# A two-stage transformer block in split fp32 on one Trainium2 core: 33 row pairs instead of 34, a re-ordered sort, two re-ordered quads, an early gelu table and a last store from ScalarE's queue

## The reference

```python
# layer 0, x: (64, 64, 512); H = 2048
q, k, v = x @ Wq, x @ Wk, x @ Wv
attn = softmax(einsum('btd,bTd->btT', q, k) * 512 ** -0.5)
attn_out = einsum('btT,bTd->btd', attn, v) @ Wp + bp
cms_out = gelu(attn_out @ cW1 + cb1) @ cW2 + cb2 + one_hot(target)[:, None, :]
modifier = gelu(concat([attn_out, cms_out]) @ mW1 + mb1) @ mW2 + mb2
x = clip(x + cms_out + modifier, 0, 1)
# layer 1, one of three roles for each batch, K = 256
h = gelu(x @ W_down[role] + b_down[role])
y = x + h @ W_up[role] + b_up[role]
out = layernorm(y) * gamma[role] + beta[role]
```

## Time and profile before

| | us |
|---|---|
| median of three runs | 2051.75 (2050.34 to 2052.19) |
| the profiled execution | 2051.32 |
| its span | 2049.7 |
| TensorE busy | 2010.7 (98%) |
| VectorE busy | 1396.4 (68%) |
| ScalarE busy | 952.6 (46%) |
| GpSimd busy | 109.3 (5%) |
| mean granted clock of TensorE | 0.997 |

### The profile page before, as it was taken

The page is one execution under the profiler, slowest core; times in us unless marked ns, Lnnn a source line. Parts: engine busy times, 40 slices in busy tenths (PEclk is TensorE's granted clock), DMA queues, the critical chain, the costliest instruction groups (busy, mean ns, idle before and its releaser), DMA issues.

```text
span 2049.7 us, 28141 instructions
## 1 busy us (share of the span) xinstructions
PE 2010.7 (98%) x9396; PEld 1674.5 (82%) x9396; DVE 1396.4 (68%) x2598; ACT 952.6 (46%) x1980; POOL 109.3 (5%) x202
## 2 busy tenths in 40 slices
PE   8999999999999999999999999999999999999996
PEld 6878888888878888888878888888878888888896
DVE  6686786555777686556686786565686685654996
ACT  4754453433654444333564453333474454342664
POOL 0000000000000000000000000000000000000132
PEclk9999999999999999999999999999999999999998
DMA  4121233315211143125111233224211222222754
GB/s 165 32 62 42 72 124 108 93 56 196 63 51 62 52 144 108 57 83 206 62 52 52 62 129 98 72 93 185 83 51 42 73 98 93 93 88 88 235 160 107
DMA packets 113408, 194.32 MB, mean 95 GB/s; under 512 B 12457, under 2 KB 72370, under 8 KB 108788
## 3 DMA queue, kind: packets, MB, share of 16 engines
q1 hardware_dynamic: 98772, 128.81, 20.1%
q0 software_dynamic: 14496, 63.72, 9.0%
HBM read 148.97 MB, written 43.52 MB: 94 GB/s over the span
## 4 chain that ended last, share of the span: by engine, by line
PE 85%; DVE 7%; SPq 2%; DMA 2%; ACT 2%; issue 2%; DVEq 0%; POOL 0%; ACTq 0%; POOLq 0%
PE y L1663 15%; PE y L1665 15%; PE y L1664 15%; PE x L1663 13%; PE x L1665 13%; PE x L1664 13%; DVE w_lo L1105 1%; PE y L1744 1%; SPq L452 1%; DVE f L1229 1%; PE x L1769 1%; SPq L460 1%; DVE a_forms L1274 1%; DMA w_blocks<-w1c 1%; DMA bet<-beta 1%
## 5 line engine op out<-in xcount | busy, mean ns | idle before, releaser
L683 ACT CAST w_hi<-w_blocks 128x512 fp32r<-128x512 f32 (+1 forms) x464 | 231.6, 519 | 132.5 <-PE y L1665 84.1
L1105 DVE TENSOR_TENSOR w_lo<-w_blocks,w_hi 128x512 fp32r<-128x512 f32 (+1 forms) x464 | 249.7, 564 | 56.2 <-ACT w_hi L683 56.2
L1663 PE MATMUL x<-h_hi,w_hi 128*128 128x512 f32 x512 | 199.6, 390 | 3.8 <-ACT f L736 3.8
L1663 PE MATMUL y<-h_hi,w_hi 128*128 128x512 f32 x512 | 199.7, 390 | 1.9 <-ACT p_copy L736 1.9
L1664 PE MATMUL x<-h_lo,w_hi 128*128 128x512 f32 x512 | 199.3, 389 | 0.0
L1665 PE MATMUL x<-h_hi,w_lo 128*128 128x512 f32 x512 | 199.2, 389 | 0.0
L1665 PE MATMUL y<-h_hi,w_lo 128*128 128x512 f32 x512 | 199.2, 389 | 0.0
L1664 PE MATMUL y<-h_lo,w_hi 128*128 128x512 f32 x512 | 199.2, 389 | 0.0
L1663 PE MATMUL y<-a_forms,w_hi 128*128 128x512 f32 x480 | 188.1, 392 | 2.2 <-DVE f L1208 1.2
L1665 PE MATMUL y<-a_forms,w_lo 128*128 128x512 f32 x480 | 186.8, 389 | 0.0
L1664 PE MATMUL y<-a_forms,w_hi 128*128 128x512 f32 x480 | 186.8, 389 | 0.0
(11 more groups left out here) (227 smaller groups left out, 4265.8 us busy)
## 6 DMA issues: line engine op xcount, KB each, us to landing
w_blocks<-w1m SPq DMA_DIRECT2D x128, 256.0 KB, 4.6
w_blocks<-w1c SPq DMA_DIRECT2D x64, 256.0 KB, 3.2
w_st<-w2c SPq DMA_DIRECT2D x64, 256.0 KB, 3.0
w_st<-w2m SPq DMA_DIRECT2D x64, 256.0 KB, 4.7
x_hi_lo<-x_halves POOLq DMA_DIRECT2D x6, 2048.0 KB, 11.1
zs<-z_by_batch SPq DMA_DIRECT2D x68, 128.0 KB, 2.1
cms<-f SPq DMA_DIRECT2D x32, 256.0 KB, 2.7
z_cms<-cms POOLq DMA_DIRECT2D x8, 1024.0 KB, 7.1
```

The source lines that it names most:

```text
L683: nc.scalar.copy(w1_hi[:, w % RING, cols], src).then_inc(w1_hi_s, 1)
L1105: nc.vector.tensor_tensor(w1_lo[:, w % RING, cols], src, f32(w1_hi[:, w % RING, cols]), ALU.subtract).then_inc(w1_lo_s, 1)
L1663: nc.tensor.matmul(ps, w[0], x[0], start=first, stop=False, skip_group_check=more)
```

## The change

Five edits.

1. Pairs. An odd batch of a role among the first 48 no longer pads its group; it moves to the group of the same role among the last 16. `NPAIR` goes from 34 to 33. The sort gets ten more small instructions. Its list is also cut in three: `sort_halves` stays, `sort_starts` goes behind two copies of the second weight product, `sort_slots` goes behind the first query tile, and `onehot_bias` goes from ahead of the first `inverse` to behind the first `split_v`.
2. The start. The first row of the first weight product takes its four hi x hi matmuls first, and these wait for the hi halves alone.
3. The two second quads. In the opening quad VectorE takes `sum_p6` and `sum_p7` ahead of P3's weight split, then `block22`, `hidden_lo` of the last C12 (until now in the attention), `block21`, and `block12` right behind the first weight split of the next quad; its `weight_sums` go forward in the attention, and ScalarE takes gelu C11 ahead of the next quad's splits. In the second quad of mW1 TensorE takes P1, P6, P7, P5 instead of P1, P5, P7, P6.
4. The gelu table. ScalarE runs one gelu of a column of 128 constants near the end of each attention. The second layer of the first quad waits for gelu C21 only where it first writes C21's bank (column block 3).
5. The last store of first rows is issued by ScalarE's queue instead of GpSimd's.

```diff
-NPAIR = B // 2 + 2 * (R // 2)
+NPAIR = B // 2 + R // 2
@@ sync, store_second
-                sp.wait_ge(a_stored[u % UNROLL], (n - u % UNROLL) * (16 // UNROLL) + 16)
+                if n == NPAIR - 1:
+                    sp.wait_ge(last_a, 16)
+                else:
+                    sp.wait_ge(a_stored[u % UNROLL], 16 * (n // UNROLL + 1))
@@ gpsimd: store_first for all pairs but the last
-            for n in range(NPAIR):
+            for n in range(NPAIR - 1):
@@ scalar, quad
                 if Q % (2 * NQ) == 1:
                     copy_p1(Q)
                     split_q(Q, P3)
+                    gelu(Q, C11)
...
-                if q:
+                if q and Q % (2 * NQ) != 1:
                     gelu(Q, C11)
@@ scalar, attention
                 output(m - 1)
+                if s == 0:
+                    act.wait_ge(mhalf_s, 1)
+                nc.scalar.activation(warm[:], mhalf[:], ACT.Gelu)
                 output_hi(m - 1)
@@ scalar, end
+            b = act.value_load(first_t[0:1, NPAIR - 1:NPAIR], min_val=0, max_val=B - 1)
+            act.wait_ge(yo_s, NPAIR)
+            act.dma_start(out[bass.ds(b, 1)].rearrange("o s d -> (o s) d"),
+                          yo[0:S, (NPAIR - 1) % UNROLL, :]).then_inc(last_a, 16)
+            act.wait_ge(last_a, 16)
@@ vector, sort_halves: +3 instructions; sort_slots: +7
+                link(nc.vector.tensor_scalar(count[:, 0:R], sort_bank[0:B, NG:NG + R], -1.0, None, ALU.add))
...
+            def sort_starts():
                 link(nc.vector.memset(start[:, 0:1], 0.0))
...
@@ vector, quad
-                if q:
-                    split_q(Q, P3)
                 if opening:
                     sum_p6(Q)
                     sum_p7(Q)
+                if q:
+                    split_q(Q, P3)
                 if opening or not q:
                     block22(Q)
+                if opening:
+                    hidden_lo(Q - 1, C12)
+                    block21(Q)
                 if (Q + 1) % NQ or Q // NQ % 2 == 0:
                     weight_sums(Q + 1)
...
                 split_next(Q, 0)
+                if opening:
+                    block12(Q)
@@ vector, attention
+                    if s == 0 and c == 0:
+                        sort_slots()
...
-                    onehot_bias()
...
                 split_v(m0)
+                if s == 0:
+                    onehot_bias()
...
                 hidden_lo(Q, C11)
+                weight_sums(Q + 1)
                 hidden_lo(Q, C21)
...
-                weight_sums(Q + 1)
...
-                hidden_lo(Q, C12)
@@ tensor, weight_product
+                    if ready + k == 0:
+                        for seen, x, y in (((qw_hi, 2), 0, 0), ((qw_lo, 1), 1, 0), ((qw_lo, 2), 0, 1)):
+                            pe.wait_ge(*seen)
+                            for m in range(DC):
+                                nc.tensor.matmul(banks[m][:], lhs[:, x, k, m * P:(m + 1) * P], rhs(k)[y],
+                                                 start=x + y == 0, stop=False)
+                        continue
@@ tensor, quad
-                for k, first_seen in zip((P1, P5, P7, P6), seen):
+                begin = list(zip((P1, P5, P7, P6), seen))
+                if q == 1 and g % 2:
+                    begin = [begin[n] for n in (0, 3, 2, 1)]
+                for k, first_seen in begin:
@@ tensor, second1
-                if q == 0:
-                    pe.wait_ge(*((part_s, 4 * Q) if g % 2 else (gelu_s, 4 * Q + C21 + 1)))
+                if q == 0 and g % 2:
+                    pe.wait_ge(part_s, 4 * Q)
...
+                        if Q % (2 * NQ) == 0 and j == 0 and c == 3:
+                            pe.wait_ge(gelu_s, 4 * Q + C21 + 1)
```

More of the change, by code:

```diff
@@ L99 @@
 NG = 2 * R
-NPAIR = B // 2 + 2 * (R // 2)
+NPAIR = B // 2 + R // 2
 NSLOT = 2 * NPAIR
+SLOTS_KNOWN = 8 + (2 * NG + 3) + NG + 11
 UNROLL = 4
@@ L144, in program @@
         ones2 = sb("ones2", [P, P], F32R)
+        warm = sb("gelu_table", [P, 1])
         mx = sb("mx", [P, 1])
@@ L181, in program @@
             half = sb("half", [B, NG], on=sorting)
+            count = sb("count", [B, NG], on=sorting)
+            spare = sb("spare", [B, R], on=sorting)
+            moved = sb("moved", [B, R], on=sorting)
+            shift = sb("shift", [B, R], on=sorting)
             start = sb("start", [B, NG], on=sorting)
@@ L332, in program @@
         rstd_s, yg_s, yo_s = sem("rstd"), sem("times_gamma"), sem("row_ready")
+        last_a = sem("last_first_stored")
         a_stored = [sem(f"first_stored{k}") for k in range(UNROLL)]
@@ L1067, in sort_halves @@
                 dve.wait_ge(sort_mm, 2)
+                link(nc.vector.tensor_scalar(count[:, 0:R], sort_bank[0:B, NG:NG + R], -1.0, None, ALU.add))
                 for r in range(NG):
-                    link(nc.vector.tensor_scalar(flags[:], even[:], sort_bank[0:B, NG + r:NG + r + 1], None, ALU.is_lt))
+                    if r == R:
+                        link(nc.vector.scalar_tensor_tensor(out=spare[:], in0=half[:, 0:R], scalar=-2.0, in1=count[:, 0:R],
+                                                            op0=ALU.mult, op1=ALU.add))
+                        link(nc.vector.scalar_tensor_tensor(out=count[:, R:NG], in0=spare[:], scalar=1.0,
+                                                            in1=sort_bank[0:B, NG + R:2 * NG], op0=ALU.add, op1=ALU.add))
+                    link(nc.vector.tensor_scalar(flags[:], even[:], count[:, r:r + 1], None, ALU.is_lt))
                     link(nc.vector.reduce_sum(half[:, r:r + 1], flags[:], AX_X))
-            def sort_slots():
+            def sort_starts():
                 link(nc.vector.memset(start[:, 0:1], 0.0))
@@ L1077, in sort_slots @@
                                                         in1=start[:, r - 1:r], op0=ALU.mult, op1=ALU.add))
+            def sort_slots():
                 link(nc.vector.tensor_tensor(rank_r[:], sort_bank[0:B, 0:NG], start[:], ALU.add))
+                link(nc.vector.scalar_tensor_tensor(out=rank_r[:, R:NG], in0=spare[:], scalar=1.0, in1=rank_r[:, R:NG],
+                                                    op0=ALU.add, op1=ALU.add))
+                link(nc.vector.scalar_tensor_tensor(out=moved[:], in0=half[:, 0:R], scalar=-2.0,
+                                                    in1=sort_bank[0:B, 0:R], op0=ALU.mult, op1=ALU.add))
+                link(nc.vector.tensor_scalar(moved[:], moved[:], 0.0, None, ALU.is_ge))
+                link(nc.vector.tensor_tensor(shift[:], start[:, R:NG], start[:, 0:R], ALU.subtract))
+                link(nc.vector.scalar_tensor_tensor(out=shift[:], in0=half[:, 0:R], scalar=-2.0, in1=shift[:],
+                                                    op0=ALU.mult, op1=ALU.add))
+                link(nc.vector.tensor_tensor(shift[:], shift[:], moved[:], ALU.mult))
+                link(nc.vector.tensor_tensor(rank_r[:, 0:R], rank_r[:, 0:R], shift[:], ALU.add))
                 link(nc.vector.tensor_tensor(rank_r[:], rank_r[:], onehot[:], ALU.mult))
@@ L1305, in quad @@
                 split_pre(pre_block(Q, 1))
-                block21(Q)
+                if not opening:
+                    block21(Q)
                 hidden_lo(Q, C11)
                 split_next(Q, 3)
-                block12(Q)
+                if not opening:
+                    block12(Q)
                 hidden_lo(Q, C21)
@@ L1557, in _ @@
             sort_halves()
-            sort_slots()
             for j in (0, 2):
@@ L1561, in _ @@
                 nc.vector.tensor_copy(h1_tile[:, j, :], Y[j][:]).then_inc(wa_out, 1)
+            sort_starts()
             for s in range(NS):
@@ L1693, in sort_gather @@
             def sort_gather():
-                pe.wait_ge(sort_v, 8 + 2 * NG + 1 + (NG - 1) + 4)
+                pe.wait_ge(sort_v, SLOTS_KNOWN)
                 for v in range(3):
@@ L1759, in output @@
                 if m == 0:
-                    pe.wait_ge(sort_v, 8 + 2 * NG + 1 + (NG - 1) + 5)
+                    pe.wait_ge(sort_v, SLOTS_KNOWN + 1)
                 elif p == 0:
```

5 lines of the change are left out of this document (2 added, 3 removed).

## The result

The changed kernel takes 2032.84 us (median of 4, 2032.40 to 2032.96), the kernel before beside it 2051.21: a ratio of 0.9907, 95% interval 0.9894 to 0.9919, 18.4 us less. The forecast was 2035.8, 2032.0 to 2041.5. The profiled executions have spans of 2049.7 and 2030.8: 18.9 less, where the sum of the forecast was 15.75 (some 0.8 of the 18.9 goes with slow load issues in the one execution of the kernel before that was profiled; see "One pair less").

What follows compares the result with a forecast made beforehand. TensorE, busy for 98% of the span, bounds the kernel, so only fewer matmuls or shorter waits help. Seven items sum to 15.75 us off 2051.3, giving 2035.6, stated as a median of 2035.8; range 2032 to 2041.5.

Steps and rivals of the forecast that it cites:

- Items 1 and 2: Start and sort: first matmuls wait for hi halves only, 0.8 us; sort links moved behind copies and query tile, 1.25 us.
- Item 3: Gelu table loaded early near each attention's end, and `second1`'s wait moved to bank 3: 0.6 us a step, 2.4 in all.
- the rival of a load twice as long: Gelu table load holds ScalarE 2 x 1.28 us: item 3 is -0.9, time 2038.9; chance 0.03.
- Item 4: Opening quad: two TensorE waits save 4.4 and 4.0 us, P5 of the next quad gives back 3.0: 5.4.
- The rival in which nothing comes back: Opening quad: `part` additions run ahead as in later quads, so item 4 is 8.4 us, time 2032.8; chance 0.2.
- Item 5: mW1's second quad: P6 and P7 ahead of P5 remove its wait for `block12`: 1.5 us, bounds 0.9 and 1.5.
- P6 and P7 first give it 5.4 us: mW1's second quad: running P6 and P7 first gives P5's wait for `block12` 5.4 us.
- The rival "slower": mW1's second quad: a ScalarE and VectorE chain behind P5 exceeds 8.2 us, deciding from 4 us excess; time 2057, chance 0.03.
- Item 6: Pairs: one fewer saves 3.6 us of TensorE plus SyncE's lag of 0.25: 3.85, between 3.3 and 3.9.
- the last pair's load is late: End of the pairs: waits run through SyncE's queue, and TensorE stands 0.60 + 0.16 us for the last load.
- Item 7: Last store of first rows on ScalarE's queue instead of GpSimd's: 0.55 us less, bounds 0 and 0.7.
- ScalarE should be like SyncE: 0.15 + 2.3 = 2.45: Last store: ScalarE's store was to start and land like SyncE's, 2.45 us instead of 3.0.

Runs made afterwards that it cites:

- One pair less: Follow-up on the changed kernel with one filler pair more, 34 again, all else as changed: 2036.56 us, ratio 0.9918 to the kernel before.
- the undone start: The changed kernel with the first row of the first weight product as before, waiting for the lo half of Wk: 2033.45 us, ratio 0.9912.
- the store alone: The kernel before with only the last store of first rows moved from GpSimd's queue to ScalarE's: 2048.47 us, ratio 0.9982.
- the old opening quad: The changed kernel with VectorE's and ScalarE's order for the opening quad of each cW1 stage as before: 2043.75 us, ratio 0.9955.
- the late lo half: The changed kernel with the opening quad's `hidden_lo` of C21 behind the next quad's `part` additions: 2031.10 us, ratio 0.9895 to the kernel before.

## Why the prediction was right, and where it was not

**Items 1 and 2** came out at 2.11 where the sum has 2.05, but not by their own terms. The first matmul is at 6.38 and not 6.2, and the undone start shows that its gain is within the spread of the clock's rise. The 0.98 at the first query tile is the earlier copies (32.53, so 1.06 earlier, where 1.3 was counted), and that tile still waits (0.43). The 1.0 at 57.43 was 1.07: this step of item 2 holds. The 0.15 that `onehot_bias` was to cost shows as 0.12 at the first output, behind the place where the 2.11 is read. No run undoes the sort's order by itself, so item 2 rests on these rows.

**Item 3** was 0.72 in each step by the offset at `second1` (0.6), and 2.70 over the stretches from the step before to P4, in which up to 0.14 is lost ahead of it. The early gelu runs 0.02 behind the end of a load of 1.28 (92.08 + 1.28, and 93.38), so the rival of a load twice as long is out. The Trainium skill ("ScalarE: Activation LUTs", What ACT_TABLE_LOAD costs) adds a drain of about 1.38 to each load; neither this row nor what follows it shows one: the gelu stands at 93.38, and ScalarE's next cast starts at 93.49.

**Item 4** had its mechanism right: the two waits gave 9.01 (8.4), and P5 of the next quad gave 2.77 back (3.0), with `part` as releaser, as named. The chain from `sum_p6` to the end of `part` takes 125.18 - 113.52 = 11.7, as forecast. By the offsets P4's wait is worth 1.04 in each step, 4.2 (4.4), and the second one 4.8 (4.0). The forecast had taken 0.4 off the latter for bank 3; that loss is real, but shows in the give-back: of the 2.77, 0.5 is bank 3, and P1 and P5 gave back 2.2, where 2.6 had been put on them. The rival in which nothing comes back names 2032.8, which is the measured time, but it is not what happened: the 2.77 came back, and other items made up for it.

**Item 5** failed. The step "P6 and P7 first give it 5.4 us" holds, and P5's wait is gone from the list, worth 0.47 in each step, 1.9. But nothing was said of P4, which comes behind P5, `second1` and P2. It waits for `sum_p7`, behind weight sums that wait for a DMA, and it took 1.05 and 0.43 back in two steps. 0.36 was left. The rival "slower" looked at this chain, but only from P5's side; its excess of 4 us never came.

**Item 6** was 4.62 (3.85): 3.7 for the pair, where 3.6 was counted, and some 0.8 for the last load's wait, of which the forecast took 0.25. The step "the last pair's load is late" read one execution as the rule: with the store alone, 34 pairs have no such wait, so the change itself is worth about 3.7.

**Item 7** was right in sign for a wrong reason. The step "ScalarE should be like SyncE: 0.15 + 2.3 = 2.45" failed: the store is issued 0.18 behind the row and lands 2.9 later, and SyncE's own store is issued at 2025.4, 3.1 behind the last row, where it was 3.0 before. That term is nothing. 2.87 came from GpSimd's drain, which the forecast had as "the closing wait of 5.8 to the end" and kept fixed. That row named TensorE's sequencer as the releaser, whose own closing instruction starts at 2034.2 and takes 1.2; the engine named had long been done, so another one held the end, and the forecast did not ask which.

Forecast 15.75, measured 18.9: item 7 gave 2.3 more, item 4 0.8, item 6 0.8, item 3 0.3 more, item 5 1.1 less. Items 3, 5, 6 and 7 all lie outside their own bounds, item 7 far outside its 0 to 0.7. That the sum stayed in the range owes something to luck: without item 7's excess of 2.3, which had nothing to do with its reason, the time would be about 2035.2, next to the forecast, and with it it is 0.8 above the range's lower end.

## What to carry to other kernels

Look at the closing instructions of every engine before you price the end: if one of them drains long behind its last work, what counts is when that engine gets its last work, until the last store's landing is the later one. A wait that is removed uncovers the next one on the same chain, so name the releaser of each later product of the quad and what that releaser itself waits for. An edit that brings TensorE earlier is worth only as much as the next engine's order lets through: price it together with that order. And a wait that one trace shows once may be that execution's own: look for it in a second trace before it is priced.

## What was not expected of the hardware

- GpSimd's closing drain takes 7.75 to 8.05 us in all fourteen traces, from its last work on, whether this is a store that has landed or a 0.55 us inverse; VectorE's takes 0.77, TensorE's 1.2 to 1.3, ScalarE's and SyncE's 0.01 behind a store of theirs. No run here shows what it does in this time.
- The landing of a weight block, issued at the same place in the program, made VectorE wait between 5.05 and 7.22 us from step to step and execution to execution. What TensorE loses by it in mW1's second quad adds up to 0.2 to 2.4 us in the eight traces with the new order.
- The rise of TensorE's clock from the pace of 1.2 GHz came 3.1 to 6.1 us after its first matmul, whatever the start looked like.
- An issue of one of SyncE's `zs` loads takes 0.34 us in the median and now and then 1.2 to 1.6 us in some executions and not in others. In the two traces above that have two such issues late (the old opening quad, the late lo half) TensorE lost 1.6 and 1.2 us in the pairs.
